# Routed experts in tiles of 256 rows, with the up weights as the standing operand, and a reordered start of the second attention

## The chip, the cores and the metric

The kernel runs on one core of one Trainium2 chip. The metric is the device time of one execution in microseconds; lower is better. The engines of the core are TensorE (PE in the profile, its weight loads PEld), VectorE (DVE), ScalarE (ACT), GpSimd (POOL) and SyncE (SP), which here only issues DMAs.

## What is computed

Two layers of a gated transformer over x of shape (16, 256, 256) in float32. Layer 0 is cross attention and then a mixture of experts; layer 1 is cross attention with a feed-forward part, and then a ternary feed-forward network. The change touches the mixture, and the start of the cross attention behind it. Cut to what matters, the mixture is:

```
scores = softmax(xt @ gate_w.T)            # xt: 4096 tokens x 256, 8 experts
top_vals, top_idx = top_k(scores, 2)
combine = sum(one_hot(top_idx) * top_vals)
for each expert (W1, B1, W2, B2, W3, B3, c):
    h = silu(xt @ W1 + B1) * (xt @ W3 + B3)
    y += c[:, None] * (h @ W2 + B2)
z = (silu(xt @ sw1 + sb1) * (xt @ sw3 + sb3)) @ sw2 + sb2     # shared expert
x = x + tanh(g_ffn[0]) * (y + z)
```

The next line of the reference is the second cross attention on layer-normed x.

## The kernel before

The kernel runs its stages one after another: attention 0, the mixture (`mixture_on_*`), attention 1, its feed-forward part, the ternary network. Each engine has its own hand-written order of steps; engines meet only through semaphores (`wait_ge`, `then_inc`). There is no planner. `paired_blocks` writes a loop: the first block, a hardware loop whose body has two blocks (so that buffers alternate), and the last ones written out.

Products are made exact enough by splitting: each operand is kept as a rounded part `hi` (fp32r) and a residue `lo`, and `product` (its three matmuls per pair are L674, L675 and L676 of the profile) adds hi*hi, lo*hi and hi*lo.

The mixture has two parts. In the shared part all 16 blocks of 256 tokens go through the shared expert, whose weights stand in TensorE while 256 tokens stream. Beside it the routing is worked out: two experts for each token, a place for each of the 8192 pairs in a list sorted by expert, the tokens of each tile (`tokens`, by 64 steps of `place` with tables of zeros and ones, `hot` on VectorE and `tile_values` on ScalarE, L1270), and the expert of each tile.

In the routed part the sorted list is worked off in 72 tiles of 128 rows (`SORTED`), 12 groups of 6 (`GROUP`). Per tile:

- GpSimd gathers 128 rows of normed x with one indirect DMA (L1189), up to 11 tiles ahead, and writes `choice` (L1198), a 128x128 operand that picks the expert's bias rows. It waits for older tiles' output before it overwrites a choice.
- TensorE transposes x (`transpose_x`, L1752), two tiles ahead. `weights` (L1757) loads the expert's column offset into a register. `up` (L1768 is its bias product) has the transposed x as standing operand and streams 512 columns of weights: 1 + 6 products. Then the gated h of the tile before is transposed (`transpose_h`, L1777), and `down` of two tiles before runs: 6 products of 256 columns and a bias product (L1787).
- ScalarE rounds x (L1336), makes silu (L1340), rounds the transposed h (L1344) and writes the output times the row's weight (L1350).
- VectorE makes x's residue (L1620), the gate product (L1631) and h's residue (L1625).
- SyncE stores a group of 6 tiles at once, the last group tile by tile (L1141).

TensorE's order in a group is `up(j)`, `transpose_h(j - 1)`, `transpose_x(j + 2)`, `down(j - 2)`. At the top of each group the loads for two older tiles and for the group's first tile stand in a row.

Attention 1 starts when all rows of `sorted_y` are stored. GpSimd gathers each token's two rows, for the first two blocks the second row into a buffer of its own (L873), which VectorE adds (`add_rows`, L476), and otherwise by adding DMAs into x (L871). A block's second gather waits for its first to land. VectorE takes statistics (L349), GpSimd makes the deviation (L858, L860), VectorE normalises (L366), TensorE transposes (L701). `keys` (L387) and `value_tails` (L397) finish keys and values, and TensorE's transposes of x wait for both the normalised x and the value tails. `late_rows` marks the first block of attention 1, in which the second block's rows are added late.

## Time and profile before

| what | us |
| --- | --- |
| median of 3 runs | 1362.4 (1361.49 to 1372.14) |
| the profiled execution, its own time | 1369.89 |
| its span in the trace | 1368.1 |
| mean granted clock of TensorE | 0.963 of full speed |
| busy: PE, DVE, ACT, POOL | 1221.4, 952.0, 779.3, 641.6 |

All durations in the prediction come from the one profiled execution. Its time is 7.5 us above the median of the three runs. An engine's busy time is the union of its instructions; matmuls overlap each other in the profile, so their pace is read from the distance of their starts.

### The profile page before, as it was taken

How to read it: one execution, taken by the hardware profiler on the slowest of the kernel's cores; microseconds unless marked ns; L12 is line 12 of the kernel's file. 1: busy time of each engine (PE TensorE's matmuls, PEld its weight loads, DVE VectorE, ACT ScalarE, POOL GpSimd, SP SyncE). 2: the span in 40 equal slices, each digit the busy share in tenths (PEclk: the TensorE clock that was granted, in tenths of full speed). 3: DMA queues.
4: the chain of work that ended last, by engine and by line, in shares of the span. 5: the costliest groups of instructions: out<-in, count | busy, mean ns of one | idle time of the engine just before them, and what ended most of it. 6: DMA issues, size and time to landing. Idle time of an engine off the chain costs nothing.

```text
span 1368.1 us, 27370 instructions
## 1 busy us (share of the span) xinstructions
PE 1221.4 (89%) x8822; PEld 1097.0 (80%) x8823; DVE 952.0 (70%) x2124; ACT 779.3 (57%) x1589; POOL 641.6 (47%) x790
## 2 busy tenths in 40 slices
PE   5999999989796899999469999998789999799998
PEld 4888888889795788888458888987678888687877
DVE  5788888766873333333448888887688778888886
ACT  3676777667383344444336777765434445466664
POOL 4333343142104444442377776730335545567776
PEclk9999999989999999999779999999899999899999
DMA  3122112123001332221333334310300000000000
GB/s 94 50 55 63 48 49 51 42 72 117 9 1 47 108 89 88 88 73 54 89 64 64 65 59 72 57 28 5 109 1 0 0 0 1 0 24 24 23 23 31
DMA packets 70041, 66.25 MB, mean 48 GB/s; under 512 B 26080, under 2 KB 62176, under 8 KB 69728
## 3 DMA queue, kind: packets, MB, share of 16 engines
q1 hardware_dynamic: 55264, 44.29, 11.2%
q0 software_dynamic: 12288, 17.83, 6.7%
q10 hardware_dynamic: 2432, 3.41, 0.8%
q8 instruction: 31, 0.51, 0.2%
q14 instruction: 26, 0.21, 0.1%
HBM read 42.43 MB, written 17.83 MB: 44 GB/s over the span
## 4 chain that ended last, share of the span: by engine, by line
PE 67%; DVE 13%; ACT 8%; issue 7%; POOL 3%; DMA 2%; another core or an unknown queue 0%; ACTq 0%; DVEq 0%; POOLq 0%
PE PSUM L674 11%; PE PSUM L676 10%; PE PSUM L675 10%; PE PSUM L746 6%; PE PSUM L725 6%; PE PSUM L734 4%; PE PSUM L689 2%; ACT s_m_xn L1270 2%; PE PSUM L744 2%; PE PSUM L2478 2%; PE PSUM L2479 2%; PE PSUM L701 1%; PE PSUM L1768 1%; PE PSUM L2470 1%; PE PSUM L2459 1%
## 5 line engine op out<-in xcount | busy, mean ns | idle before, releaser
L1930 POOL TENSOR_TENSOR s_f_h_lo<-s_f_h,s_f_h_hi 128x512 fp32r<-128x512 f32 x64 | 87.1, 1369 | 110.9 <-ACT s_f_h_hi L1897 110.8
L1631 DVE TENSOR_TENSOR s_m_h<-PSUM,s_m_h 128x256 f32<-128x256 f32 x72 | 30.6, 425 | 148.1 <-ACT s_m_h L1340 147.1
L746 PEld LDWEIGHTS PSUM<-s_a_v_diagonal,s_a_prob_t 128*128 128x128 f32 x1024 | 127.5, 194 | 0.0
L746 PE MATMUL PSUM<-s_a_v_diagonal,s_a_prob_t 128*128 128x36 f32 x1024 | 126.6, 270 | 0.0
L871 POOL DMA_INDIRECT s_x<-sorted_y,s_slots x60 | 95.2, 1587 | 51.7 <-DMA s_x<-sorted_y,s_slots 36.1
L409 DVE TENSOR_REDUCE s_a_row_max<-PSUM 128x8 f32<-128x640 f32 x128 | 104.3, 815 | 14.1 <-PE PSUM L725 10.4
L1189 POOL DMA_INDIRECT s_m_xn<-normed_x,s_tokens x72 | 70.1, 973 | 89.5 <-DVE s_tokens L1497 77.0
L623 ACT ACTIVATE s_a_prob_t<-PSUM 128x640 f32<-128x640 f32 x128 | 89.5, 699 | 33.6 <-PE PSUM L734 32.9
L416 DVE TENSOR_TENSOR s_a_less<-PSUM,s_a_row_max 128x640 f32<-128x640 f32 x128 | 105.0, 820 | 3.6 <-issue 0.2
L606 ACT ACTIVATE s_a_prob<-s_a_less 128x512 f32<-128x512 f32 x128 | 80.5, 629 | 44.4 <-DVE s_a_less L416 42.0
L725 PE MATMUL PSUM<-s_a_kd,s_a_q_hi 64*128 64x320 f32 x512 | 91.0, 360 | 13.6 <-DVE s_a_q_lo L379 12.7
L1894 ACT ACTIVATE s_f_h<-PSUM,s_cols 128x512 f32<-128x512 f32 x64 | 44.0, 687 | 96.0 <-PE PSUM L676 93.6
L734 PE MATMUL PSUM<-s_ident,s_a_prob 128*128 128x128 f32 x640 | 94.6, 279 | 2.8 <-ACT s_a_prob L607 2.3
L616 ACT ACTIVATE PSUM<-s_a_mask 128x640 f32<-128x640 f32 (+1 forms) x128 | 89.4, 699 | 0.0
L2307 POOL TENSOR_TENSOR s_t_gh<-s_t_h,s_t_g 128x1024 f32<-128x1024 f32 x32 | 78.1, 2442 | 21.7 <-ACT s_t_h L2268 21.7
L883 POOL TENSOR_TENSOR s_x<-s_x,s_a_bias 128x512 f32 (+1 forms) x16 | 20.3, 1270 | 144.5 <-DVE s_a_xn L366 133.9
L1340 ACT ACTIVATE s_m_h<-PSUM 128x256 f32<-128x256 f32 x72 | 27.6, 383 | 98.4 <-PE PSUM L676 89.5
L1198 POOL TENSOR_TENSOR s_m_x_hi<-s_m_bias,s_ones 128x128 fp32r<-128x128 f32 x72 | 28.6, 399 | 115.4 <-PE PSUM L1787 113.6
L674 PE MATMUL PSUM<-s_ffn_hi,s_f_h_hi 128*128 128x256 f32 x256 | 74.0, 289 | 6.7 <-POOL s_f_h_lo L1930 6.6
L734 PEld LDWEIGHTS PSUM<-s_ident,s_a_prob 128*128 128x128 f32 x640 | 76.8, 151 | 3.6 <-issue 3.6
L674 PE MATMUL PSUM<-s_moe_w,s_m_h_hi 128*128 (+1 forms) x208 | 67.7, 325 | 12.4 <-DVE s_x L1517 5.4
L725 PEld LDWEIGHTS PSUM<-s_a_kd,s_a_q_hi 64*128 64x128 f32 x512 | 48.8, 186 | 30.2 <-issue 15.1
(309 smaller groups left out, 4359.3 us busy)
## 6 DMA issues: line engine op xcount, KB each, us to landing
sorted_y<-s_m_xn SPq DMA_DIRECT2D x11, 768.0 KB
s_a_kd<-s_a_k_parts SPq DMA_DIRECT2D x256, 20.0 KB
s_x<-x SPq DMA_DIRECT2D x16, 256.0 KB, 2.7
s_a_ctx<-ctx SPq DMA_DIRECT2D x32, 128.0 KB
s_moe_raw<-moe_w SPq DMA_DIRECT2D x16, 256.0 KB
normed_x<-s_m_xn SPq DMA_DIRECT2D x16, 256.0 KB, 3.3
y<-s_x SPq DMA_DIRECT2D x16, 256.0 KB, 2.1
s_late_raw<-moe_w SPq DMA_DIRECT2D x11, 256.0 KB, 3.0
```

The lines of the kernel that those rows point to most:

```text
L409: dve.tensor_reduce(mx, s, AX.X, ALU.max).then_inc(a.max_done, 1)
L416: dve.tensor_tensor(a.prob[j % 2][:].rearrange("p (c h) n -> p c h n", c=2), s, mx.unsqueeze(3).broadcast_to([P, 2, HPC // 2, CTXP]), ALU. ...
L616: act.activation(a.scores[:, j % 2, :, 0:HPC // 2 * CTXP].rearrange("p c (h n) -> p c h n", n=CTXP), mask.unsqueeze(1).broadcast_to([P, 2, ...
L623: act.activation(a.prob_t[j % 2][:], a.prob_t_ps, ACT.Copy).then_inc(a.pt_done, 1)
L674: pe.matmul(ps, lh, rh, start=start and i == 0, stop=False, skip_group_check=not start)
L675: pe.matmul(ps, ll, rh, start=False, stop=False, skip_group_check=not start)
L676: last = pe.matmul(ps, lh, rl, start=False, stop=stop and i == n - 1, skip_group_check=not start)
L725: last = pe.matmul(ps, queries[i][rows, m, qt * P:(qt + 1) * P], keys[i][rows, m], start=False, stop=i == 2, skip_group_check=True)
L734: last = pe.transpose(a.prob_t_ps[:, c, :], a.pairs[j % 2][:, c, :], ident[:])
L746: last = pe.matmul(a.o_ps[:, 2 * c:2 * c + 2, :], a.prob_t[j % 2][:, c, :], v[:, j // BT, 0, 2 * c:2 * c + 2], start=False, stop=c == PC - ...
L871: last = pool.indirect_dma_start(x[:, tile, :], None, d["sorted_y"], row, compute_op=ALU.add)
L1930: pool.tensor_tensor(f.h_lo[m % 4][:], f.h[m % 4][:], f.h_hi[m % 4][:].bitcast(F32), ALU.subtract).then_inc(f.h_split, 1)
```

## The change

- A routed tile has 256 rows (`BT` = 2 gathers and halves per tile). There are `ROUTED` = 32 + 8 - 1 = 39 tiles, 13 groups of 3 (`GROUP`); tables of half tiles have 78 columns, not 72.
- `copy_up` on VectorE: a register load of the tile's expert, then a copy of its up weights (128 x 2048, hi and lo) into one of two buffers `up_w`. It waits until the product that used the buffer is done.
- `up` now has these weights as standing operand and streams x: 24 products of 256 columns into one of two pairs of PSUM banks. h comes out transposed; `transpose_h` and its steps are gone.
- The bias of up is no longer a product: `up_biases` makes a table for all tiles by four products once, and ScalarE and VectorE add it per partition.
- `down` makes two halves of 6 + 1 products; x, h, and output are rounded and split 256 rows at a time, by the forms that the shared part uses. `choice` serves `down` alone.
- TensorE's order is `transpose_x(j + 1)`, `up(j)`, `down(j - 1)`. Its loop has 6 tiles per turn. ScalarE, VectorE and SyncE have their 39 tiles written out; each tile is stored by itself. Gathers run two tiles ahead; the choice of tile n and the gathers of tile n + 2 alternate.
- The loads of attention 1's weights go out after the fourth tile's store.
- In attention 1 GpSimd splits the second context before the first deviation and issues both gathers of the third block ahead of the first turn. On VectorE `keys` and `value_tails` come ahead of the late rows in the first turn, and the third block's statistics at its end.

TensorE in the hardware loop, around `down`. Before (L674 to L676 with `s_m_x_hi` are up products of 512 columns, with `s_m_h_hi` down products; L1777 transposes h, L1752 x; `s_m_expert` holds the offsets):

```order
L676 MATMUL PSUM<-s_moe_w,s_m_x_hi 128x512
L1774 REGISTER_ALU
L1777 MATMUL PSUM<-s_ident,s_m_h 128x128 x2
L83 REGISTER_ALU
L1752 MATMUL PSUM<-s_ident,s_m_xn 128x128 x2
L674 ISA
L674 MATMUL PSUM<-s_moe_w,s_m_h_hi 128x256
L675 MATMUL PSUM<-s_moe_w,s_m_h_lo 128x256
```

Now (the same products are L677 to L679, `s_m_up_w` is the copied weight):

```order
L677 MATMUL PSUM<-s_m_x_hi,s_m_up_w 128x256
L678 MATMUL PSUM<-s_m_x_hi,s_m_up_w 128x256
L679 MATMUL PSUM<-s_m_x_lo,s_m_up_w 128x256
L1757 ISA
L1757 TENSOR_LOAD s_m_expert
L1757 ISA x2
L1783 REGISTER_ALU
L677 ISA
L677 MATMUL PSUM<-s_moe_w,s_m_h_hi 128x256
L678 MATMUL PSUM<-s_moe_w,s_m_h_lo 128x256
```

Between the last up product and the first down product stood four transposes; now a register load stands there, and the transposes of x follow `down`.

VectorE in a routed tile, before (gate, h's residue, x's residue of one half each):

```order
L1631 TENSOR_TENSOR s_m_h<-PSUM,s_m_h 128x256
L1625 TENSOR_TENSOR s_m_h_lo<-PSUM,s_m_h_hi 128x2x128
L1620 TENSOR_TENSOR s_m_x_lo<-PSUM,s_m_x_hi 128x2x128
L1631 TENSOR_TENSOR s_m_h<-PSUM,s_m_h 128x256
L1625 TENSOR_TENSOR s_m_h_lo<-PSUM,s_m_h_hi 128x2x128
```

Now:

```order
L1611 TENSOR_LOAD s_m_expert
L1611 ISA x2
L1612 ISA
L1612 COPY s_m_up_w<-s_moe_w 128x2048
L1606 TENSOR_TENSOR s_m_x_lo<-PSUM,s_m_x_hi 128x512
L1617 SCALAR_TENSOR_TENSOR s_m_h<-PSUM,s_m_bias,s_m_h 128x256 x2
L1623 TENSOR_TENSOR s_m_h_lo<-s_m_h,s_m_h_hi 128x512
```

A register load and a copy of 2048 elements head each tile's row, ahead of x's residue and the gate; h's residue now reads SBUF, not PSUM.

VectorE in the first turn of attention 1, before (L476 adds the second block's rows, L349 with the following L357 are statistics, L387 and L397 keys and value tails):

```order
L416 TENSOR_TENSOR s_a_less<-PSUM,s_a_row_max 128x640
L476 TENSOR_TENSOR s_x<-s_x,s_z_sum 128x512
L349 BN_STATS s_a_stats<-s_x 128x6 x2
L357 BN_AGGR s_a_mv<-s_a_stats 128x2 x2
L366 TENSOR_SCALAR s_a_xn<-s_x,s_a_mv,s_a_rstd 128x256 x2
L349 BN_STATS s_a_stats<-s_x 128x6 x2
L387 SCALAR_TENSOR_TENSOR s_a_k_parts<-PSUM,s_cols,s_a_k_parts 128x80 x2
L397 TENSOR_TENSOR s_a_v_diagonal<-PSUM,s_headmask 64x2x4x16 x2
```

Now:

```order
L416 TENSOR_TENSOR s_a_less<-PSUM,s_a_row_max 128x640
L387 SCALAR_TENSOR_TENSOR s_a_k_parts<-PSUM,s_cols,s_a_k_parts 128x80 x2
L397 TENSOR_TENSOR s_a_v_diagonal<-PSUM,s_headmask 64x2x4x16 x2
L476 TENSOR_TENSOR s_x<-s_x,s_z_sum 128x512
L349 BN_STATS s_a_stats<-s_x 128x6 x2
L357 BN_AGGR s_a_mv<-s_a_stats 128x2 x2
L366 TENSOR_SCALAR s_a_xn<-s_x,s_a_mv,s_a_rstd 128x256 x2
L409 TENSOR_REDUCE s_a_row_max<-PSUM 128x8
```

Keys and tails moved up before the added rows, and the third block's statistics left this place; they stand at the end of the turn.

The diff, cut to its core:

```diff
-CHOICES = 4
-SORTED = 2 * TILES + EXPERTS
-GROUP = 6
-GROUPS = SORTED // GROUP
+CHOICES = 2
+ROUTED = TILES + EXPERTS - 1
+SORTED = BT * ROUTED
+COLUMNS = ROUTED + ROUTED % 2
+GROUP = 3
+GROUPS = ROUTED // GROUP
...
+                if ahead > 1 and not late_rows:
+                    ln_stats(b.next().next())
+                if ahead:
+                    keys(b.next())
+                if ahead:
+                    value_tails(b.next())
                 if late_rows:
                     add_rows(second)
                     ln_stats(second)
                     ln_aggregate(second)
                     ln_apply(second)
-                if ahead > 1:
-                    ln_stats(b.next().next())
-                if ahead:
-                    keys(b.next())
-                if ahead:
-                    value_tails(b.next())
                 if behind:
...
+                if late_rows:
+                    ln_stats(second.next())
+                    ln_aggregate(second.next())
...
                 gather(first, 1, a.second_rows[0])
+                split_context(second)
                 inverse_std(first)
                 gather(second, 0)
                 gather(second, 1, a.second_rows[1])
-                split_context(second)
                 gather(third, 0)
+                gather(third, 1)
...
-                    gather(third, 1)
...
+            for n in range(ROUTED):
+                sp.wait_ge(m.y_done, SHARED + n + 1)
+                sp.dma_start(sorted_y[:, BT * n:BT * (n + 1), :], m.tile_y[n % 2][:]).then_inc(m.tile_out[n % 2], 16)
+                if n == GROUP:
+                    for i in WA_ORDER:
+                        sp.dma_start(a1.w_raw[:, i], d["wa1"][:, i]).then_inc(a1.w_in[i], 16)
...
+                after(pool, m.t_ps, SHARED + n - 1 if n > 1 else 0)
+                for t in range(BT):
+                    pool.indirect_dma_start(m.tile_x[n % 2][:, t, :], None, d["normed_x"],
+                                            bass.IndirectOffsetOnAxis(ap=tokens[:, BT * n + t:BT * n + t + 1], axis=0)
+                                            ).then_inc(m.tile_in[n % 2], 16)
...
+            gather(0)
+            gather(1)
+            for n in range(ROUTED):
                 choose(n)
+                if n + 2 < ROUTED:
+                    gather(n + 2)
...
+            def output(n):
+                act.wait_ge(m.y_ps, SHARED + n + 1)
+                after(act, m.tile_out[n % 2], 16 * (n // 2))
+                for t in range(BT):
+                    last = act.activation(m.tile_y[n % 2][:, t, :], m.routed_y_bank[n % 2][:, t], ACT.Copy,
+                                          scale=m.tile_weight[:, BT * n + t:BT * n + t + 1])
+                last.then_inc(m.y_done, 1)
+
+            x_rounded(0)
+            for n in range(ROUTED):
+                if n + 1 < ROUTED:
+                    x_rounded(n + 1)
+                activate(n)
+                if n:
+                    output(n - 1)
+                h_rounded(n)
+            output(ROUTED - 1)
...
+            def up_biases():
+                dve.wait_ge(m.logits_ps, BATCH + 2)
+                dve.tensor_copy(m.up_bias, m.up_bias_ps)
...
+            def copy_up(n):
+                after(dve, m.up_done, SHARED + n - 1 if n > 1 else 0)
+                at_expert = dve.value_load(m.expert[0:1, n:n + 1], min_val=EXPERT_COLS, max_val=EXPERTS * EXPERT_COLS)
+                dve.tensor_copy(m.up_w[n % 2][:], m.w[:, bass.ds(at_expert, 4 * MOE_CHUNK)]).then_inc(m.up_copied, 1)
+
+            def gate(n):
+                dve.wait_ge(m.silu_done, SHARED + n + 1)
+                for o in range(KC):
+                    last = dve.scalar_tensor_tensor(m.h[n % 2][:, o], m.routed_up_ps[n % 2][:, 1, o], m.up_bias[:, KC + o, n:n + 1],
+                                                    m.h[n % 2][:, o], ALU.add, ALU.mult)
+                last.then_inc(m.gated, 1)
+
+            def h_residue(n):
+                dve.wait_ge(m.h_round, SHARED + n + 1)
+                dve.tensor_tensor(m.h_lo[n % 2][:], m.h[n % 2][:], m.h_hi[n % 2][:].bitcast(F32),
                                   ALU.subtract).then_inc(m.h_split, 1)
 
+            up_biases()
+            dve.wait_ge(m.late_split, LATE_CHUNKS)
+            copy_up(0)
+            copy_up(1)
+            x_residue(0)
+            for n in range(ROUTED):
+                if n and n + 1 < ROUTED:
+                    copy_up(n + 1)
+                if n + 1 < ROUTED:
+                    x_residue(n + 1)
+                gate(n)
+                h_residue(n)
...
+            def up_biases():
+                pe.wait_ge(m.slots_done, 3)
+                for o in range(4):
+                    last = pe.matmul(m.up_bias_ps[:, o, :], m.bias_parts[:, o * P:(o + 1) * P], m.chosen_r[:], start=True, stop=True)
+                last.then_inc(m.logits_ps, 1)
...
+            def up(g, j):
+                z = (g.z + j) % 2
                 n = GROUP * g.n + j
+                pe.wait_ge(m.up_copied, n + 1)
+                pe.wait_ge(m.t_split, n + 1)
+                after(pe, m.gated, SHARED + n - 1)
+                hi, lo = ([m.up_w[z][:, (2 * k + lower) * MOE_CHUNK:(2 * k + lower + 1) * MOE_CHUNK] for k in range(KC)] for lower in range(2))
+                for gate in range(2):
+                    for o in range(KC):
+                        cut = slice(gate * DIM + o * P, gate * DIM + (o + 1) * P)
+                        last = product(pe, m.routed_up_ps[z][:, gate, o], [(hi[k][:, cut], lo[k][:, cut], m.x_hi[z][:, k], m.x_lo[z][:, k])
+                                                                          for k in range(KC)])
+                last.then_inc(m.up_done, 1)
+
+            def down(g, j):
+                z = (g.z + j) % 2
+                n = GROUP * g.n + j
+                w = weights(g, j)
+                hi, lo = (part(w, 2 * KC + lower).rearrange("p (k c) -> p k c", k=KC) for lower in range(2))
                 pe.wait_ge(m.chosen_done, n + 1)
                 pe.wait_ge(m.h_split, SHARED + n + 1)
+                pe.wait_ge(m.y_done, SHARED + n - 1)
+                for t in range(BT):
+                    tile = slice(t * P, (t + 1) * P)
+                    product(pe, m.routed_y_bank[z][:, t], [(m.h_hi[z][:, k, tile], m.h_lo[z][:, k, tile], hi[:, k], lo[:, k])
+                                                           for k in range(KC)], stop=False)
+                    last = pe.matmul(m.routed_y_bank[z][:, t], m.choice[z][:], m.bias_parts[:, 2 * DIM:], start=False, stop=True)
+                last.then_inc(m.y_ps, 1)
 
             pe.wait_ge(m.x_split, BATCH)
             pe.wait_ge(m.late_split, LATE_CHUNKS)
+            up_biases()
+            transpose_x(Block(0, 0, 0), 0)
 
             def tiles_of(g, behind, ahead):
                 for j in range(GROUP):
+                    at(g, j + 1, behind, ahead, transpose_x)
+                    up(g, j)
+                    at(g, j - 1, behind, ahead, down)
+
+            paired_blocks(pe, GROUPS, tiles_of, 0, 2)
+            down(final_group, GROUP - 1)
```

## Rows read from the trace of the kernel before

**Rows 1.** The page, busy time of each engine over the whole span.

```profile
PE 1221.4 (89%) x8822; PEld 1097.0 (80%) x8823; DVE 952.0 (70%) x2124; ACT 779.3 (57%) x1589; POOL 641.6 (47%) x790
```

**Rows 2.** Timeline of the routed stage's start and end (start us, us, engine, line, operation).

```profile
428.34 0.95 POOL L1189 DMA_INDIRECT s_m_xn<-normed_x,s_tokens  x1 [0.30 <-issue]
...
429.26 0.75 DVE L1517 SCALAR_TENSOR_TENSOR s_x<-PSUM,s_gates,s_x 128x512 f32<-128x512 f32 x1 [2.08 <-PE PSUM L1697]
...
434.92 0.79 PE L1768 MATMUL PSUM<-s_m_bias_parts,s_m_x_hi 128*128 128x512 f32 x1 [3.06 <-POOL s_m_x_hi L1198]
...
664.81 0.47 ACT L1350 ACTIVATE s_m_xn<-PSUM,s_m_bias 128x256 f32<-128x256 f32 x1 [1.38 <-PE PSUM L1787]
```

**Rows 3.** Windows, 540 to 560 us (window: length, busy per engine, clock, DMA share, GB/s).

```profile
540.00:560.00 20.00, 19.57 (x122) 16.97 (x121) 6.69 (x20) 9.29 (x27) 9.67 (x15) 1.00 0.28 90
```

**Rows 4.** Timeline of TensorE, one routed tile at 540 us.

```profile
540.32 0.40 PE L676 MATMUL PSUM<-s_moe_w,s_m_x_hi 128*128 x1
...
541.25 0.38 PE L1777 MATMUL PSUM<-s_ident,s_m_h 128*128 128x128 f32 x2
...
541.47 0.38 PE L1752 MATMUL PSUM<-s_ident,s_m_xn 128*128 128x128 f32 x2
...
541.92 0.28 PE L676 MATMUL PSUM<-s_moe_w,s_m_h_hi 128*128 x1
...
542.40 0.28 PE L1787 MATMUL PSUM<-s_m_bias_parts,s_m_x_hi 128*128 128x256 f32 x1
...
543.21 0.39 PE L676 MATMUL PSUM<-s_moe_w,s_m_x_hi 128*128 x1
```

**Rows 5.** Timeline, idle time before an instruction in the routed stage, in brackets.

```profile
448.87 0.47 ACT L1350 ACTIVATE s_m_xn<-PSUM,s_m_bias 128x256 f32<-128x256 f32 x1 [3.22 <-remote]
...
478.13 0.47 PE L1768 MATMUL PSUM<-s_m_bias_parts,s_m_x_hi 128*128 128x512 f32 x1 [0.43 <-DVE s_m_x_lo L1620]
...
496.96 0.47 PE L1768 MATMUL PSUM<-s_m_bias_parts,s_m_x_hi 128*128 128x512 f32 x1 [1.26 <-POOL s_m_x_hi L1198]
```

**Rows 6.** Timeline of the shared experts' stage: silu, gate, h rounded, h's residue, 256 rows each.

```profile
423.13 0.81 ACT L1253 ACTIVATE s_m_h<-PSUM,s_cols 128x256 f32<-128x256 f32 x2
...
423.98 0.88 DVE L1522 SCALAR_TENSOR_TENSOR s_m_h<-PSUM,s_cols,s_m_h 128x256 f32<-128x256 f32 x2 [3.19 <-ACT s_m_h L1253]
...
424.89 0.63 ACT L1259 ACTIVATE s_m_h_hi<-s_m_h 128x512 fp32r<-128x512 f32 x1 [0.95 <-DVE s_m_h L1522]
...
425.55 0.69 DVE L1528 TENSOR_TENSOR s_m_h_lo<-s_m_h,s_m_h_hi 128x512 fp32r<-128x512 f32 x1 [0.70 <-ACT s_m_h_hi L1259]
```

**Rows 7.** Timeline around 990 us: VectorE's 128x2048 operation, with GpSimd busy and idle.

```profile
988.27 2.20 DVE L2223 TENSOR_SCALAR s_t_code<-s_t_raw 128x2048 fp32r<-128x2048 f32 x1
...
994.15 1.23 DVE L2223 TENSOR_SCALAR s_t_code<-s_t_raw 128x2048 fp32r<-128x2048 f32 x1
...
987.65 1.73 POOL L1930 TENSOR_TENSOR s_f_h_lo<-s_f_h,s_f_h_hi 128x512 fp32r<-128x512 f32 x1 [1.76 <-ACT s_f_h_hi L1897]
```

**Rows 8.** GpSimd's gather and choice: the gather's own answer, the page's group.

```profile
L1189 POOL DMA_INDIRECT s_m_xn<-normed_x,s_tokens x72: 942/969/1200, 426.8 to 622.6; - x72
...
DMA to landing us min/median/max: 3.0/3.0/3.0
...
L1198 POOL TENSOR_TENSOR s_m_x_hi<-s_m_bias,s_ones 128x128 fp32r<-128x128 f32 x72 | 28.6, 399 | 115.4 <-PE PSUM L1787 113.6
```

**Rows 9.** The register load of an expert's offset on TensorE's queue.

```profile
L1757 PEldq TENSOR_LOAD <-s_m_expert x96: 296/301/1240, 431.5 to 662.2; - x96
```

**Rows 10.** Windows with the granted clock (the number before the DMA share).

```profile
448.00:452.00 4.00, 2.41 (x9) 2.32 (x10) 1.09 (x3) 1.77 (x5) 1.77 (x3) 0.50 0.16 52
...
708.00:712.00 4.00, 4.00 (x20) 3.34 (x19) 1.92 (x4) 0.70 (x1) 3.69 (x4) 0.50 0.49 85
```

**Rows 11.** Timeline of the second attention's first turn, TensorE and VectorE.

```profile
704.90 1.09 PE L701 MATMUL PSUM<-s_ident,s_a_xn 128*128 128x128 f32 x4 [11.07 <-DVE s_a_v_diagonal L397]
...
702.96 0.75 DVE L349 BATCH_NORM_STATS2 s_a_stats<-s_x 128x6 f32<-128x256 f32 x2 [5.02 <-DMA s_x<-sorted_y,s_slots]
```

More of the change, by code:

```diff
@@ L984, in __init__ @@
                 self.h_lo = [sb(scope, f"m_h_lo{z}", [P, KC, SEQ], F32R) for z in two]
-                self.tile_x = [self.xn[:, z * GROUP:(z + 1) * GROUP, :] for z in two]
-                self.tile_y = [self.xn[:, (2 + z) * GROUP:(3 + z) * GROUP, :] for z in two]
-                self.choice = [self.x_hi[z // KC][:, z % KC, P:] for z in range(CHOICES)]
                 def by_token(buffer):
@@ L1121, in mixture_on_sync @@
                     load_late(n + 2)
-            def store(g):
-                sp.wait_ge(m.y_done, SHARED + GROUP * (g.n + 1))
-                sp.dma_start(sorted_y[:, bass.ds(GROUP * g.n, GROUP), :], m.tile_y[g.z]).then_inc(m.tile_out[g.z], 16)
-            sp.wait_ge(m.y_ps, SHARED + GROUP)
-            for i in WA_ORDER:
-                sp.dma_start(a1.w_raw[:, i], d["wa1"][:, i]).then_inc(a1.w_in[i], 16)
-            def body(g, behind, ahead):
-                if behind:
-                    store(g.last())
             sp.wait_ge(m.late_split, LATE_CHUNKS)
@@ L1346, in output @@
-            def output(g, j):
-                act.wait_ge(m.y_ps, SHARED + GROUP * g.n + j + 1)
-                if j == 0:
-                    after(act, m.tile_out[g.z], 16 * g.half)
-                act.activation(m.tile_y[g.z][:, j, :], m.y_ps_bank[:, 0], ACT.Copy,
-                               scale=m.group_weight[g.z][:, j:j + 1]).then_inc(m.y_done, 1)
-            act.wait_ge(m.up_done, SHARED)
-            for j in range(AHEAD):
-                x_rounded(Block(0, 0, 0), j)
-            def tiles_of(g, behind, ahead):
-                for j in range(GROUP):
-                    activate(g, j)
-                    at(g, j - 1, behind, ahead, h_rounded)
-                    at(g, j + AHEAD, behind, ahead, x_rounded)
-                    at(g, j - 2, behind, ahead, output)
@@ L1628, in gate @@
-            def gate(g, j):
-                dve.wait_ge(m.silu_done, SHARED + GROUP * g.n + j + 1)
-                h = m.h[j % 2][:, 0]
-                dve.tensor_tensor(h, m.tile_up_ps[:, j % 2, DIM:], h, ALU.mult).then_inc(m.gated, 1)
-            for j in range(AHEAD):
-                x_residue(first, j)
-            def tiles_of(g, behind, ahead):
-                for j in range(GROUP):
-                    gate(g, j)
-                    at(g, j - 1, behind, ahead, h_residue)
-                    at(g, j + AHEAD, behind, ahead, x_residue)
@@ L1761, in part @@
                 return m.w[:, bass.ds(at + n * MOE_CHUNK, MOE_CHUNK)]
-            def up(g, j, w):
+            def up(g, j):
+                z = (g.z + j) % 2
                 n = GROUP * g.n + j
-                pe.wait_ge(m.chosen_done, n + 1)
-                pe.wait_ge(m.t_split, n + 1)
-                ps = m.tile_up_ps[:, j % 2, :]
-                pe.matmul(ps, m.choice_of(g, j), m.bias_parts[:, 0:2 * DIM], start=True, stop=False, skip_group_check=True)
-                product(pe, ps, [(m.x_hi[j % 2][:, k, 0:P], m.x_lo[j % 2][:, k, 0:P], part(w, 2 * k), part(w, 2 * k + 1))
-                                 for k in range(KC)], start=False).then_inc(m.up_done, 1)
@@ L1772, in transpose_h @@
-            def transpose_h(g, j):
-                n = GROUP * g.n + j
-                pe.wait_ge(m.gated, SHARED + n + 1)
-                pe.wait_ge(m.h_split, SHARED + n)
-                for k in range(KC):
-                    last = pe.transpose(m.ht_bank[:, k], m.h[j % 2][:, 0, k * P:(k + 1) * P], ident[:])
-                last.then_inc(m.ht_ps, 1)
-            def down(g, j, w):
-                n = GROUP * g.n + j
-                hi, lo = (part(w, 2 * KC + n).rearrange("p (k c) -> p k c", k=KC) for n in range(2))
-                pe.wait_ge(m.h_split, SHARED + n + 1)
-                pe.wait_ge(m.y_done, SHARED + n)
-                product(pe, m.y_ps_bank[:, 0], [(m.h_hi[j % 2][:, k, 0:P], m.h_lo[j % 2][:, k, 0:P], hi[:, k], lo[:, k])
-                                                for k in range(KC)], stop=False)
-                pe.matmul(m.y_ps_bank[:, 0], m.choice_of(g, j), m.bias_parts[:, 2 * DIM:], start=False, stop=True).then_inc(m.y_ps, 1)
+                pe.wait_ge(m.up_copied, n + 1)
@@ L1789, in mixture_on_tensor @@
             pe.wait_ge(m.x_split, BATCH)
-            pe.wait_ge(m.slots_done, 3)
             pe.wait_ge(m.late_split, LATE_CHUNKS)
-            for j in range(AHEAD):
-                transpose_x(Block(0, 0, 0), j)
+            up_biases()
+            transpose_x(Block(0, 0, 0), 0)
             def tiles_of(g, behind, ahead):
-                offset = {j: weights(g.last(), j + GROUP) for j in (-2, -1) if behind}
                 for j in range(GROUP):
-                    offset[j] = weights(g, j)
-                    up(g, j, offset[j])
-                    at(g, j - 1, behind, ahead, transpose_h)
-                    at(g, j + AHEAD, behind, ahead, transpose_x)
-                    at(g, j - 2, behind, ahead, lambda group, tile: down(group, tile, offset[j - 2]))
```

140 lines of the change are left out of this document (56 added, 84 removed).

## Prediction

> **What bounds the kernel now.** I read the page first, then the stretch of routed tiles by windows, one tile of it in the timeline, the idle gaps of TensorE there, and last the first microseconds of the second attention.
>
> The page says that TensorE is busy 89% of the span [rows 1]. That is a mean over stages with different limits. The change touches the routed stage, from the first up product at 434.92 us to the last row of experts' output at 664.81 + 0.47 = 665.28 us [rows 2], and the start of the second attention. From 540 to 560 us TensorE is busy 19.57 of 20 us, VectorE 6.69, ScalarE 9.29 and GpSimd 9.67 [rows 3]: the stage is bound by TensorE's stream, and the other three have more than half their time free.
>
> One routed tile of 128 rows, in the timeline: the same product of two tiles starts at 540.32 and 543.21, so a tile takes 2.89 us [rows 4]. The busy times of single matmuls overlap, so I count distances of starts. From 540.32 to 541.25 TensorE starts four products of 512 columns, 0.232 us each; from 541.92 to 542.40 four of 256, 0.12 each (0.1175 over longer runs); from 541.25 to 541.47 is 0.22 us for a pair of transposes. Seven wide products (1.62), seven narrow ones (0.82) and two pairs of transposes (0.44) make 2.88 us, which agrees. 72 such tiles are 207.7 us. The stage lasts 230.4. The other 22.7 us are gaps and low clock: some 3 us in which TensorE waits for an output of ScalarE that starts at 448.87 after 3.22 us of waiting, 1.26 and 0.43 us at the starts of groups, where three register loads stand in a row (496.96 and 478.13 stand for twelve such places, some 9 us in all) [rows 5], a stretch at half clock before and after, and the drain.
>
> **The change, part by part.**
>
> *TensorE's work per tile.* A tile now has 256 rows and there are 39 instead of 72. Up: 4 output parts x 6 products of 256 columns = 24; down: 2 x 7 = 14; x transposed: 4 transposes; no h transposes and no bias product with the up part. 38 x 0.1175 + 0.44 = 4.91 us per tile, x 39 = 191.4 us (less 0.9 for two sets of transposes ahead of the first product: 190.6). Against 207.7 this is -17.1 us. Most of it is transposes (4 per 128 rows before, 2 now) and the bias products; the column count hardly moves, since 78 half tiles stand where 72 stood.
>
> *Does another engine become the bound?* With T the tile time, E the end of up(n) on TensorE, and durations from [rows 6]: silu of two halves 0.81 us ends at E+0.9; gate 0.88 ends at 1.8; ScalarE must first put out tile n-1, which waits for down(n-1) (E+1.65) and takes 0.9, so h is rounded from 2.7 to 3.3; h's residue 0.69 ends at 4.1. down(n) starts on TensorE at E+4.91, so 0.8 us are spare. Then VectorE goes on: weight copy, x residue 0.69, next gate. VectorE's own ring is copy + 0.69 (x) + 0.88 (gate) + 0.10 + 0.63 + 0.10 (wait for the rounding on ScalarE) + 0.69 (h) = copy + 3.1 us.
>
> *The copy.* 2048 elements per partition, SBUF to SBUF, and the trace of before has no such copy. Nearest rows: a TENSOR_SCALAR of 128x2048 with fp32r output takes 1.23 us at 994.15, when GpSimd is idle, and took 2.20 at 988.27, when it started while GpSimd's TENSOR_TENSOR ran until 989.38 [rows 7]. I take 1.23, the row without company. [...] With 1.23 the ring is 4.33 us, below 4.91. [...]
>
> GpSimd's share: one choice 0.40 and two gathers of 0.97 with 0.3 between, 2.9 us per tile, and it starts a gather for tile n+2 as soon as tile n is transposed. Landing takes 3.0 us [rows 8], so both are there 0.5 + 1.27 + 3.0 = 4.8 us later, and are used about 9.4 us later. This cover of 4.6 us also holds if each is pushed by a whole copy. In the steady state the second gather of a pair ends at about E+4.4 and the copy is due at E+4.1: it may lose 0.3 us. Ring: 4.6.
>
> *Register loads on VectorE.* A load of the expert's offset costs TensorE's sequencer 0.30 us and some register steps after it [rows 9]; TensorE hides one per tile behind queued matmuls. On VectorE it comes while the h residue (0.69) still runs. I take 0 exposed, bound 0.5. With that bound the ring is 5.1 us. TensorE's own load now stands before down, one per tile and not three in a row, so the gaps of [rows 5] shrink to that of the loop branch. I take 0.4 x 5 turns of the loop = 2 us instead of the 9.
>
> *Start.* Tile 0 needs two gathers instead of one. The second starts at 428.34 and lands at about 431.4; transposes, 0.63, 0.69 give 433.5. VectorE is busy with add(15) until 430.0 [rows 2], then the biases (0.2), two loads and two copies (2 x 1.23 + 0.5), so x's residue ends near 434.1 and up(0) starts at about 434.4: 0.5 earlier than now, where it waits for the choice on GpSimd. After this pause the clock is at its half level (the product at 434.92 takes 0.79 us [rows 2], and one later in the stage 0.40 [rows 4]); that costs 1.5 us as now.
>
> *The stall before 449.6.* ScalarE waits 3.22 us for something the profile calls remote [rows 5], then the granted clock is 0.50 for a while [rows 10]; together 3.0 + 2.6 = 5.6 us. Nothing in the code asks for it. ScalarE's code is now straight instead of a loop, so it may go or come again elsewhere. In the sum against the profiled run I let 2 us return.
>
> *End.* After the last up product: h chain 4.1, less down(37) 1.65, is 2.4 us exposed, then down(38) 1.65 and the output 0.94 + 0.2.
>
> Sum: 434.4 + 190.6 + 1.5 (clock) + 0.5 (first turns) + 2 (loop) + 2.4 + 1.1 (last output) + 2 = 634.5 us, against 665.28: -30.8 us. The last store is twice as large (256 KB): +0.4. In the shared stage, the one-hot tables grow from 72 to 78 columns, on VectorE, ScalarE and in 64 products: +0.7.
>
> *Second attention.* Now TensorE stands idle 11.07 us until 704.90 [rows 11]. It waits for the value tails; these stand on VectorE behind statistics of the third block, which wait 5.02 us for a gather, and this gather stands on GpSimd behind the second block's normalisation. In the new order keys and tails come right after the scores (about 694.6) and the statistics at the end of the turn. What is late next: x of the second block. GpSimd now issues the third block's second gather before the second's deviation, and must wait for the landing of the first: 693.7, two times 1.86 gives 697.1; deviation 1.0; bias 1.25 until 699.3; then VectorE normalises 0.73, and transposes start at 700.2. That gives -4.7. Later the third block's statistics come at about 714.3, deviation until 715.3, where now the normalisation is at 717.9: there only 2.6 are left. I take -3.5 (bounds -2 and -7, the latter if the shorter pause also shortens the half clock around 708 us [rows 10]).
>
> Total: -30.8 + 0.4 + 0.7 - 3.5 = -33.2 us. The profiled run took 1369.9 us (span 1368.1), the median of three is 1362.4, with two runs at 1361.5 and 1362.4. The 5.6 us stall is the most irregular thing in the profile and about as large as this difference; if the faster runs lack it, the change cannot take it from them. I count half: 1362.4 - 33.2 + 3.8 = 1333.
>
> **Rivals.**
>
> A. VectorE's ring is a little too long (register load and waits for gathers exposed): T = 5.1 to 5.3, so + 0.2 to 0.4 x 39 = 8 to 15 us: about 1345. For: the ring is only 0.3 to 0.6 below T. Against: each exposed part must occur on every tile.
>
> [...]
>
> [...]
>
> D. The loop does what it says, but the half clock appears inside it, since stalls come back as at 449: two such stalls more cost 11 us: 1344.
>
> **How the numbers follow.** Forecast 0.62, A 0.18, B 0.08, C 0.04, D 0.08. Differences above 1% (13.6 us) can be told from none. Faster by over 1% (below 1348.8): the forecast, A, D and a part of B, 0.88. Within 1%: the rest of B and a very late A, 0.08. Slower: 0.04. Range: low end, the stall gone in full, the clock better in the attention, 1333 - 10 = 1323; high end between A and B, 1350.
>
> **What would show it.** Right: tiles 4.9 us apart on TensorE, VectorE's copy 1.2 us, VectorE about 3.6 us busy per tile; no wait of TensorE for x_lo or h_lo; TensorE's pause before the second block's transposes 6 us instead of 11. [...] Were tiles 4.9 us apart and the total still above 1350, the loss would be after 665 us.

## The result and the profile after

The changed kernel takes 1356.9 us in the median of 20 runs (1354.6 to 1361.7), the kernel before 1362.1 beside it (20 runs). The ratio is 0.9957, 95% interval 0.9941 to 0.9972: 5.2 us faster by the medians, where 29 were forecast, and 7 us above the top of the range. The profiled run has its own time 1357.3 us and a span of 1355.5.

The page's busy row, to compare with [rows 1], and its group of the gathers, to compare with [rows 8]:

```profile
PE 1213.1 (89%) x9168; PEld 1112.4 (82%) x9169; DVE 1005.4 (74%) x2105; ACT 783.4 (58%) x1535; POOL 654.6 (48%) x751
...
L1182 POOL DMA_INDIRECT s_m_tile_x<-normed_x,s_tokens x78 | 98.7, 1265 | 93.4 <-DVE s_tokens L1477 75.8
```

TensorE has 8 us less to do and the share is the same 89%, so something now leaves it idle. A gather takes 1265 ns on GpSimd instead of 973. The window of [rows 3] now reads:

```profile
540.00:560.00 20.00, 18.38 (x153) 17.77 (x152) 13.12 (x20) 9.40 (x22) 10.87 (x11) 1.00 0.37 103
```

TensorE is idle 1.6 of 20 us in a stretch in which it was idle 0.4; no other engine is busy more than 13.1. So it is a wait, not a new bound. The list of waits from 430 to 655 us names it (who waited for whom; us in total, times, longest; only waits over 0.15 us are listed):

```profile
POOL s_m_choice L1188 <- PE PSUM L1789: 86.9, 37, 6.5
...
PE PSUM L1752 <- DMA s_m_tile_x<-normed_x,s_tokens: 17.7, 23, 2.6
```

TensorE's transposes of x (L1752) wait 23 times for gathered rows. One of these waits, 1.9 us, comes before the first product; 22 waits, 15.8 us, are inside the loop. The timeline of one tile, all engines, shows where they begin:

```profile
542.78 0.28 PE L1789 MATMUL PSUM<-s_m_bias_parts,s_m_choice 128*128 128x256 f32 x1
...
543.15 0.40 POOL L1188 TENSOR_TENSOR s_m_choice<-s_m_bias,s_ones 128x128 fp32r<-128x128 f32 x1 [1.54 <-PE PSUM L1789]
543.54 0.65 PE L1752 MATMUL PSUM<-s_ident,s_m_tile_x 128*128 128x128 f32 x4 [0.47 <-DMA s_m_tile_x<-normed_x,s_tokens]
543.69 0.98 POOL L1182 DMA_INDIRECT s_m_tile_x<-normed_x,s_tokens  x1
...
544.98 1.59 POOL L1182 DMA_INDIRECT s_m_tile_x<-normed_x,s_tokens  x1 [0.30 <-issue]
545.22 1.23 DVE L1612 CAST s_m_up_w<-s_moe_w 128x2048 fp32r x1
...
549.39 0.65 PE L1752 MATMUL PSUM<-s_ident,s_m_tile_x 128*128 128x128 f32 x4 [0.68 <-DMA s_m_tile_x<-normed_x,s_tokens]
```

Read it from top to bottom. Down of tile n-2 ends (542.78 + 0.28). Only then does GpSimd make the choice of tile n (543.15), and behind it, in its order, the two gathers of tile n+2 (543.69, 544.98). The second runs beside VectorE's copy and takes 1.59 us instead of 0.98. The transposes at 543.54 are those of tile n+1. Those of tile n+2 (549.39) need the rows just gathered and wait 0.68 us. The gathers were free to start when the transposes of tile n had ended, near 538.6; they started 5 us later, because an instruction with another reason to wait stood ahead of them.

The stage now goes from its first up product to its last output at 653.89 + 0.84 = 654.73 us:

```profile
433.72 0.55 PE L677 MATMUL PSUM<-s_m_x_hi,s_m_up_w 128*128 128x256 f32 x1 [0.43 <-issue]
...
653.89 0.84 ACT L1335 ACTIVATE s_m_tile_y<-PSUM,s_m_bias 128x256 f32<-128x256 f32 x2 [4.20 <-PE PSUM L1789]
```

That is 221.0 us, where before had 230.4 [rows 2] and the prediction 200.1 (634.5 less 434.4). The second attention's pause, which was 11.07 us [rows 11]:

```profile
690.03 1.11 PE L704 MATMUL PSUM<-s_ident,s_a_xn 128*128 128x128 f32 x4 [6.09 <-DVE s_a_xn L366]
```

### The profile page after: what moved, and what is told of

It is laid out like the page before. It is cut to its first block, busy times and chain, and to the rows that moved or that the text cites. A ratio compares the mean times of both kernels' runs of the same rounds, so it can differ in the third digit from the quotient of the medians.

```text
span 1355.5 us, 27131 instructions
## 1 busy us (share of the span) xinstructions
PE 1213.1 (89%) x9168; PEld 1112.4 (82%) x9169; DVE 1005.4 (74%) x2105; ACT 783.4 (58%) x1535; POOL 654.6 (48%) x751
## 4 chain that ended last, share of the span: by engine, by line
PE 60%; DVE 12%; ACT 7%; issue 7%; DMA 7%; POOL 5%; ACTq 0%; SPq 0%; DVEq 0%; POOLq 0%
PE PSUM L677 10%; PE PSUM L679 9%; PE PSUM L678 9%; PE PSUM L749 6%; PE PSUM L728 6%; DMA s_m_tile_x<-normed_x,s_tokens 5%; PE PSUM L737 4%; PE PSUM L692 2%; ACT s_m_xn L1252 2%; PE PSUM L747 2%; PE PSUM L2474 2%; PE PSUM L2475 1%; PE PSUM L704 1%; PE PSUM L758 1%; POOL s_m_tile_x L1182 1%
## 5 line engine op out<-in xcount | busy, mean ns | idle before, releaser
L1182 POOL DMA_INDIRECT s_m_tile_x<-normed_x,s_tokens x78 | 98.7, 1265 | 93.4 <-DVE s_tokens L1477 75.8
L677 PE MATMUL PSUM<-s_m_x_hi,s_m_up_w 128*128 128x256 f32 x312 | 92.2, 296 | 0.4 <-issue 0.4
L679 PE MATMUL PSUM<-s_m_x_lo,s_m_up_w 128*128 128x256 f32 x312 | 88.9, 285 | 0.0
L678 PE MATMUL PSUM<-s_m_x_hi,s_m_up_w 128*128 128x256 f32 x312 | 88.9, 285 | 0.0
L677 PE MATMUL PSUM<-s_ffn_hi,s_f_h_hi 128*128 128x256 f32 x256 | 73.9, 289 | 6.6 <-POOL s_f_h_lo L1926 6.6
L1323 ACT ACTIVATE s_m_h<-PSUM,s_m_bias 128x256 f32<-128x256 f32 x78 | 32.7, 471 | 75.3 <-PE PSUM L679 75.3
L677 PE MATMUL PSUM<-s_moe_w,s_m_h_hi 128*128 (+1 forms) x220 | 64.9, 295 | 10.1 <-DVE s_x L1503 5.3
```

What stands on the lines that cost most here:

```text
L677: pe.matmul(ps, lh, rh, start=start and i == 0, stop=False, skip_group_check=not start)
L678: pe.matmul(ps, ll, rh, start=False, stop=False, skip_group_check=not start)
L679: last = pe.matmul(ps, lh, rl, start=False, stop=stop and i == n - 1, skip_group_check=not start)
L1182: pool.indirect_dma_start(m.tile_x[n % 2][:, t, :], None, d["normed_x"], bass.IndirectOffsetOnAxis(ap=tokens[:, BT * n + t:BT * n + t + 1] ...
```

## The experiments

Three theories. W: the choice's wait holds back the gathers behind it. L: beside VectorE's copy the second gather takes 1.59 us instead of 0.98 (called the lock here), and this makes it late. D: the landings themselves are late (up to 6.3 us, 3.4 in the median), because stores and loads stand in the DMA engines.

The kernel before, run beside each kernel, was not always equally fast: 1368.4 us beside e1 to e4, 1362.8 beside r_after, r_gather_first, e5 and e6, 1366.6 beside r2 and e7 to e9. Only times within one of these three groups are compared to a microsecond.

**Gathers ahead of the choice (e1).**

```diff
             for n in range(ROUTED):
-                choose(n)
                 if n + 2 < ROUTED:
                     gather(n + 2)
+                choose(n)
```

> The changed kernel with the gathers of tile n+2 ahead of the choice of tile n on GpSimd; nothing else. Theory W (waiting in line: the choice waits for the end of down(n-2), and the gathers behind it in GpSimd's order begin only there, 5.4 us before they are needed, in a tile time of 5.03): gathers start at the end of the transposes of tile n, some 4.5 us earlier; TensorE's waits for the gathered rows, 15.8 us in 22 places after the first tile, go to under 2 us, all tiles stand 5.03 us apart, the whole is 14 to 16 us faster than the changed kernel, about 1342 us. Theory D (the landings themselves are late, up to 6.3 us, since stores and loads of weights stand in the DMA engines): only the short waits go, the long ones (2.6, 1.5, 1.8 us) stay, 8 us faster, 1349. Theory L (the second gather is 0.6 us longer beside VectorE's copy, and this makes the waits): its length of 1.6 us stays, and the gain is also there, since the cover is longer; e2 tells L from W.

Measured: 1335.8 us, ratio to before 0.9768 (0.9738 to 0.9797). Waits of TensorE for gathered rows inside the loop: none. The gathers now follow the transposes, and from the fourth tile on all tiles stand 4.96 us apart (timeline, first GpSimd, then TensorE):

```profile
542.23 0.40 POOL L1188 TENSOR_TENSOR s_m_choice<-s_m_bias,s_ones 128x128 fp32r<-128x128 f32 x1 [1.55 <-PE PSUM L1789]
542.85 0.98 POOL L1182 DMA_INDIRECT s_m_tile_x<-normed_x,s_tokens  x1 [0.22 <-PE PSUM L1752]
544.13 1.50 POOL L1182 DMA_INDIRECT s_m_tile_x<-normed_x,s_tokens  x1 [0.30 <-issue]
...
541.98 0.60 PE L1752 MATMUL PSUM<-s_ident,s_m_tile_x 128*128 128x128 f32 x4
...
546.94 0.60 PE L1752 MATMUL PSUM<-s_ident,s_m_tile_x 128*128 128x128 f32 x4
```

The second gather is still 1.50 us long and nobody waits for it. It went further than W's 14 to 16 us; a direct comparison follows below.

**No copies (e2).** From the third tile on only 4 of the 2048 columns are copied, so the output is wrong in part.

```diff
-                dve.tensor_copy(m.up_w[n % 2][:], m.w[:, bass.ds(at_expert, 4 * MOE_CHUNK)]).then_inc(m.up_copied, 1)
+                width = 4 * MOE_CHUNK if n < 2 else 4
+                dve.tensor_copy(m.up_w[n % 2][:, 0:width], m.w[:, bass.ds(at_expert, width)]).then_inc(m.up_copied, 1)
```

> The changed kernel with its order on GpSimd, but from the third tile on the copy of the up weights is 4 columns wide instead of 2048 (the weights of the first two tiles are used for all, so the output of the experts is left wrong in part). Theory L: the second gather of each tile falls from 1.59 to 0.98 us and lands 0.6 us sooner; the short waits of TensorE (0.3 to 0.7 us, 19 of them) vanish, of the long ones 4 to 5 us stay: about 11 us faster than the changed kernel, 1346 us. Theory W alone (the lock has no part): the second gather stays at 1.59 or, where it shortens, waits shrink by no more than 3 us. If VectorE's ring were the bound (rival A of the prediction) the tile time of tiles that do not wait would fall below 5.03 us; I expect it to stay at 5.03.

Measured: 1350.3 us, ratio 0.9873 (0.9843 to 0.9902). The changed kernel did not run beside it (elsewhere 1356.9 and 1358.1), so the gain is read from the profiled runs: from the first up product to the end of the last output 213.9 us instead of 221.0, so 7 us. Gathers from 540 to 640 us take 1009 ns, and of the waits from 440 to 640 us these are left:

```profile
L1182 POOL DMA_INDIRECT s_m_tile_x<-normed_x,s_tokens x34 | 34.3, 1009 | 7.6 <-issue 5.2
...
PE PSUM L1753 <- DMA s_m_tile_x<-normed_x,s_tokens: 10.5, 11, 2.8
```

Half the waits went, those left are longer, and the tiles without a listed wait still take 5.0 to 5.1 us, nearly all. So L is a part: it took the last 0.5 us of a cover that was nearly nothing. By itself it does not make the waits, since 10.5 us of them are left without it. The 11 us expected were too many, since the chain down, choice, gathers, landing still closes with hardly a margin.

**The changed kernel and the gathers-first kernel side by side.**

> The changed kernel again, beside the others on one chip. The first four runs had a chip on which the kernel before took 1368 us instead of 1362; the changed kernel's ratio to before was 0.9957 elsewhere. I expect 0.994 to 0.997 of before; the old attention order (0.9938 in its run) would otherwise look faster than the new.

> The gathers ahead of the choice, again, now beside the changed kernel on the same chip: 20 to 25 us faster than it (waits 15.8, tile time 4.96 instead of 5.03 for 38 tiles 2.7, half clock after the long wait 1.3, and what the earlier start gives). If the 32 us against before were a matter of the chip, the ratio to before would come back to about 0.985.

Measured: 1358.1 us (ratio 0.9971, 0.9953 to 0.9989) and 1333.6 us (0.9795, 0.9761 to 0.9828) beside 1362.8 for before. The order of two lines is worth 24.5 us. In these profiled runs the stage's last output starts 23.8 us earlier:

```profile
630.72 0.84 ACT L1335 ACTIVATE s_m_tile_y<-PSUM,s_m_bias 128x256 f32<-128x256 f32 x2 [2.88 <-PE PSUM L1789]
```

**The copy made twice (e5).** With the gathers first:

```diff
+                dve.tensor_copy(m.up_w[n % 2][:], m.w[:, bass.ds(at_expert, 4 * MOE_CHUNK)]).then_inc(m.up_first, 1)
+                dve.wait_ge(m.up_first, n + 1)
                 dve.tensor_copy(m.up_w[n % 2][:], m.w[:, bass.ds(at_expert, 4 * MOE_CHUNK)]).then_inc(m.up_copied, 1)
```

> The gathers ahead of the choice, and each tile's copy of the up weights made twice (the second waits for the first, then both are the same): what VectorE's ring has to spare. By the prediction's ring (4.33 us without waits, 4.6 with the wait for a gather) the tile time becomes 5.6 to 5.9 us instead of 4.96, 25 to 37 us slower than with one copy. If the ring has more to spare than the prediction says (VectorE's waits of 0.5 and 1.06 us per tile are slack in full), it stays under 5.3 us, under 13 us slower. [...]

Measured: 1359.7 us, 26 more than with one copy. From 440 to 640 us TensorE waits for x's residue, which stands behind the copies on VectorE, and VectorE itself is idle 0.3 us before each first copy, where the register load stands:

```profile
DVE s_m_up_w L1613 <- issue: 8.8, 32, 0.5
PE PSUM L677 <- DVE s_m_x_lo L1607: 7.2, 20, 0.5
```

VectorE's ring is then the bound. The transposes of one tile and the next stand 5.2 to 5.8 us apart, 5.53 in the mean of 32 tiles (456.39 to 633.31), and the second copy adds 1.26 us to the ring (542.47 to 543.73), so the ring with one copy is about 4.3 us: the 4.33 without waits, below the 4.6 with them. The timeline also shows the lock from both sides, GpSimd's gathers first, then VectorE's copies:

```profile
541.55 2.27 POOL L1183 DMA_INDIRECT s_m_tile_x<-normed_x,s_tokens  x1 [0.30 <-issue]
...
547.00 0.95 POOL L1183 DMA_INDIRECT s_m_tile_x<-normed_x,s_tokens  x1 [0.30 <-issue]
...
542.47 1.23 DVE L1613 CAST s_m_up_w<-s_moe_w 128x2048 fp32r x1 [0.33 <-issue]
...
548.03 1.23 DVE L1613 CAST s_m_up_w<-s_moe_w 128x2048 fp32r x1 [0.30 <-issue]
```

The first gather meets a copy before it is done and ends at 543.82, 0.12 us behind the copy's end (543.70). The second is done at 547.95, before its copy starts, and takes 0.95. The copy is 1.23 in both cases.

**The weight loads of attention 1 later (e6).** In the changed kernel:

```diff
-                if n == GROUP:
+                if n == 15:
```

> The changed kernel with the four loads of attention 1's weights after the 16th tile's store instead of the 4th's. Theory D for the longest wait: the gather issued at 460.62 us landed after 6.3 us because the four loads of 256 KB were issued at 460.01. Then the wait of 2.6 us at 466.96 goes to a short one (0.4 us) and a wait of about 2.6 us appears 12 tiles later, near 525 us; the whole stays the same within 2 us. If the long wait has another cause it stays at 466.96.

Measured: 1359.3 us, as the changed kernel (1358.1 beside it). The long wait left 466.96 us (the wait nearest to it, at 468.94, is 0.82) and came back behind the loads, which now go out at 524.53 (SyncE's queue, then TensorE):

```profile
524.53 1.91 SPq L1136 DMA_DIRECT2D s_a_w_raw<-wa  x4
...
531.91 0.48 PE L1752 MATMUL PSUM<-s_ident,s_m_tile_x 128*128 128x128 f32 x1 [3.66 <-DMA s_m_tile_x<-normed_x,s_tokens]
```

So D is shown for the single longest wait. Three waits of 0.9, 1.5 and 1.8 us at 495.5, 593.0 and 638.6, whose gathers landed late too (after 4.4, 4.5 and 5.6 us), were not tried by themselves. And a late landing needs a short cover to do harm: in r_gather_first the gather that starts at 460.17 lands after 6.3 us, and nobody waits for it. In the changed kernel the gather that started 0.6 us behind the four loads of 256 KB landed after 6.3 us, the median one after 3.4. How loads and gathers share the DMA engines was not shown.

**The order of attention 1.** Undone in the changed kernel (e3), alone in the kernel before (e4), and undone with the gathers first (e7, beside r2, the kernel that it starts from). The edit is the part of the diff on attention 1, backward or alone.

> The changed kernel with the order of before in attention 1 (both engines: rows, statistics, keys and tails on VectorE; context split, gathers of the third block on GpSimd). My theory: 3 to 4.5 us slower than the changed kernel, since TensorE's pause before the second block's transposes is 11 us again instead of 6.0: about 1360.5 us. Rival: the time comes back later in the attention, and the order is worth under 1 us.

> The kernel before with the new order of attention 1 alone. My theory: 3 to 4.5 us faster than before (1358.5 us), which leaves only about 2 us of the measured 5 to the whole change of the routed tiles in the median, although the routed stage is 10.5 us shorter in the profiled runs: the profiled run of before was 8 us above its median. Rival: the order is worth under 1 us, and the routed tiles gave all 5.

> The gathers ahead of the choice, once more, only as the kernel that the other three of this call start from: 0.976 to 0.981 of before.

> The gathers ahead of the choice, with the order of before in attention 1. The two runs on this order disagree (undoing it in the changed kernel 0 to 3 us by the medians, 1 us behind the last output in the profiled runs; alone in the kernel before 4.9 us, 3.6 us in the profiled runs). My prediction's term was 3.5 (2 to 7). If it holds, this kernel is 3 to 4.5 us slower than the one it starts from; if most of it is given back in later blocks, 0.5 to 1.5 us slower.

Measured: e3 1359.8 (ratio 0.9938, 0.9917 to 0.9960), e4 1364.4 (0.9964, 0.9949 to 0.9979), r2 1335.9 (0.9772, 0.9747 to 0.9797), e7 1336.9 (0.9783, 0.9764 to 0.9801). The changed kernel did not run beside e3, which looks better than it by the ratio and 1.7 to 2.9 us worse by the time: this pair says nothing to 0.3%. Two pairs ran side by side: e4 is 3.9 us faster than before (1368.4), r2 is 1.0 us faster than e7. The traces of e7 and r2 show where the gain goes:

```profile
672.17 1.09 PE L701 MATMUL PSUM<-s_ident,s_a_xn 128*128 128x128 f32 x4 [11.01 <-DVE s_a_v_diagonal L397]
...
690.03 0.66 PE L701 MATMUL PSUM<-s_ident,s_a_xn 128*128 128x128 f32 x4
...
705.67 0.66 PE L701 MATMUL PSUM<-s_ident,s_a_xn 128*128 128x128 f32 x4
```

```profile
668.75 1.12 PE L704 MATMUL PSUM<-s_ident,s_a_xn 128*128 128x128 f32 x4 [6.09 <-DVE s_a_xn L366]
...
688.56 0.63 PE L704 MATMUL PSUM<-s_ident,s_a_xn 128*128 128x128 f32 x4 [0.78 <-DVE s_a_v_diagonal L397]
...
704.78 0.66 PE L704 MATMUL PSUM<-s_ident,s_a_xn 128*128 128x128 f32 x4
```

These are the transposes of the second, third and fourth block, old order (e7), then new (r2). From the end of the last output (632.61 and 633.50) they start after 39.6, 57.4 and 73.1 us in the old order and 35.3, 55.1 and 71.3 in the new: a gain of 4.3, then 2.4, then 1.8 us, and at the end of the span 0.3. Before and e4 give 4.3 us at the second block and 3.6 at the end. Over all profiled runs, the time from the end of the last output to the end of the span is 699.0 to 700.8 us in the ten with the new order (mean 700.0; e9 left out) and 700.9, 701.7 and 702.9 in the three with the old one (mean 701.8). So the order is worth something, about 1.8 us by the means; single pairs scatter from 0.3 to 3.6.

**No copies, with the gathers first (e8).** The edits of e1 and e2 together.

> The gathers ahead of the choice, and from the third tile on copies of 4 columns (weights of the first two tiles used for all, so part of the experts' output is wrong). What copy and lock cost once the gathers have their cover: nothing. The second gather falls from 1.50 to 0.98 us, the tile time stays 4.96 us, the whole the same within 2 us. If the copies still cost (a VectorE ring that is nearly the bound), tiles come to 4.9 us or less and the whole is 3 us or more faster.

Measured: 1334.1 us, 0.9766 (0.9745 to 0.9787), beside 1335.9 for r2. Tiles stand 4.96 us apart, as with copies; the gathers fell to one length:

```profile
L1182 POOL DMA_INDIRECT s_m_tile_x<-normed_x,s_tokens x70 | 67.9, 970 | 19.8 <-issue 10.7 <-PE PSUM L1753 9.1
```

Once the gathers have their cover, copy and lock cost nothing that can be measured (1.8 us between the medians, while the five runs of each kernel spread over 5 to 8 us).

**A bias added between two gathers (e9).** In attention 1, with the gathers first:

```diff
                 gather(third, 0)
+                add_bias(first)
                 gather(third, 1)
...
-                if a.stage == 1 and not behind:
-                    add_bias(first)
```

> The gathers ahead of the choice, and in attention 1 GpSimd adds the first block's bias between the two gathers of the third block, while it waits 2.6 us for the first of them, instead of behind the second block's deviation, where VectorE's normalisation waits for it. The second block's transposes start 1.2 to 1.7 us earlier, the pause before them falls from 6.1 to about 4.5 us; 1 to 2 us faster at most, which the times alone can hardly show.

Measured: 1334.3 us, 0.9761 (0.9736 to 0.9785), beside 1335.9. The pause before the second block's transposes is 4.79 us instead of 6.09, near the 4.5 expected; the times alone can't tell it from nothing. No kernel of these runs beats the gathers ahead of the choice by more than that.

## Why the prediction was wrong

| | forecast | changed kernel | gathers first (e1) |
|---|---|---|---|
| first up product | 434.4 | 433.72 | 432.22 |
| tile time without a wait | 4.91 | 5.02 | 4.96 |
| listed waits for gathers in the loop | 0 | 15.8 | 0 |
| first up product to end of last output | 200.1 | 221.0 | 200.3 |
| pause before second block's transposes | 6 | 6.09 | 6.13 |
| median of all runs | 1333 | 1356.9 | 1335.8 |

*The step that failed* is GpSimd's share: "it starts a gather for tile n+2 as soon as tile n is transposed", with landing 4.8 us later, use 9.4 us later and "this cover of 4.6 us". I read the gather's own condition and not what stands ahead of it on its engine. The choice of tile n waits for down(n-2), one up and one down behind the transposes of tile n. From there to the landing are 0.1 + 0.4 + 0.14 (543.06 to 543.69), 1.29 to the second gather, 3.4 to its landing (median): 5.3 us, and the rows are due after 5.0. The cover of 4.6 us was -0.3. A tile that waits 0.4 us gives the next one as much more time, so waits of 0.3 to 0.7 come on about every second tile (intervals 5.0 and 5.5 to 5.6); with four longer ones that is the 15.8 us. [Rows 8] had shown the choice of before idle 113.6 us behind TensorE's product L1787, so the wait was in sight. In the kernel before it held nothing back, since gathers ran many tiles ahead.

That one step carries the miss: with it undone, 1333.6 and 1335.8 us against a forecast of 1333. The traces also say where the time lies. From the transposes of the third tile to those of the last are 201.0 us in the changed kernel and 178.9 in e1, 22.1 less. The listed waits are 15.8 of them. Each of the 22 costs some 0.2 more than its entry (a tile with an entry of 0.47 takes 5.59, not 4.96 + 0.47), 4.1 in all; after a wait the four transposes take 0.41 instead of 0.35 us, which is the whole difference between tiles of 5.02 and 4.96, 0.7 in all for the tiles that don't wait; the half clock behind the longest wait (granted 0.52 from 467 to 470 us) costs 1.4.

That e1 met the forecast so closely is in part luck. In its stage of 200.3 us for 200.1 the 2 us for the loop and the 2 us for the stall did not come, and 38 x 0.05 us of tile time, some 0.7 more than forecast at the start (granted clock 0.50 from 432 to 436 us) and 1.3 of half clock at the end (0.57 from 628 to 632) made up for them. Another run of the same kernel (r_gather_first), without that half clock (1.00 from 628 to 632) and with less of it at the start (0.51 from 434 to 436, then 1.00), has a stage of 197.5 us.

The other steps:
- TensorE's work, 4.91 us a tile: 4.96. The transposes with the first product behind them take 0.56 us, as forecast (0.44 + 0.12). The rest lies in the up products: from the second to the last of a tile 22 steps take 2.62 us, 0.119 each where the sum has 0.1175.
- The copy, 1.23 us: 1.23 in nearly all of 39, the longest 1.46. Right. B in the chances, and in the upper end of the range (1350), stands for a copy of 2.3 us; no run shows one. The copy's register load was taken at 0 and costs next to nothing here (VectorE is idle ahead of 3 of the 39 copies, 1.2 us in all); the 0.3 us of e5 show only where VectorE is the bound.
- VectorE's ring, 4.33 to 4.6: about 4.3, by the doubled copy. Right, and rival A is out: no tile waits for a copy (0.8 us once).
- The lock. I put its price on the copy, as 0.3 us of VectorE's ring. It fell on the other side: the second gather takes 1.58 to 1.60 us instead of 0.98 on nearly every tile, and one of the 39 copies is longer (1.46 us at 524.38, where the gather takes 1.04). "This cover also holds if each is pushed by a whole copy" would have been true of a cover of 4.6.
- The stall, "I let 2 us return", as irregular: wrong twice. The profiled run of e4, with the routed part of before, has it again (3.21 us at 445.98) and the same 230.4 us of stage, so it belongs to that code; none of it is in the changed kernel. So taking half of the profiled run's 7.5 us above the median for it had no ground, though it came out near.
- Register loads at the loop's turns, 2 us: none to be seen; with the gathers first 4.96 holds through all turns.
- The end: 2.4 us of exposed h chain are there (2.32), but after it, in the profiled run of the changed kernel, the last down part runs at half clock (granted clock 0.60 from 650 to 654 us), products 0.21 us apart instead of 0.12, 1.3 us. In its second profiled run (r_after, granted clock 1.00 from 650 to 654 us) and in one of three with the gathers first (r_gather_first, 1.00 from 628 to 632) it did not.
- Second attention: the pause of 6 is 6.09 and the -4.7 at the second block -4.3; -3.5 in the whole is about -1.8 by the means above, and 0.3 to 3.6 by the pairs. A part of the gain is given back in the blocks behind, as the prediction said, but more of it than the 1.2 us it took off.

C in the chances stands for tiles of 6.9 us, with each copy behind a whole gather. No run shows that: tiles without a wait took 5.02 us, and the copy started beside a running gather, which took 0.6 us longer. Rival D's half clock inside the loop came once in the changed kernel, behind the longest wait (transposes at 466.96, next tile 6.33 us; granted clock 0.52 from 467 to 470 us). In e6 it moved with that wait (0.50 from 532 to 535, 1.00 from 467 to 470). Behind the waits of 1.5 and 1.8 us at 593.0 and 638.6 the changed kernel's clock was 1.00.

## What to carry to other kernels

For a DMA that is to be hidden, add up the time from the last instruction *ahead of it on its engine*, whatever that one waits for, and not from its own condition. A small operation that is due late, put in front of a prefetch, takes the prefetch's whole lead (here 4.6 us by the forecast, -0.3 as measured); putting the prefetch first cost nothing here. A wait of a few tenths on every second step is worth looking for: between the two orders TensorE's busy share differs by one point (89 and 90% of the span), the time by 24 us.

## What was not expected of the hardware

A gather on GpSimd beside VectorE's fp32r copy of 2048 columns ended just behind the copy, as three pairs show: started 0.24, 0.16 and 0.92 us before the copy, it ended 0.12, 0.11 and 0.12 us after the copy's end (546.57 and 546.45; 545.63 and 545.52; 543.82 and 543.70), though it needs 0.98 us in all. By this count the first two had 0.74 and 0.82 us of work left when the copy began, and all but 0.12 us of it ran beside the copy. In all three the gather began first, and the copy still took the 1.23 us that it takes without one. One pair of the changed kernel went the other way: the gather that starts at 523.77 took 1.04 us, and the copy that starts 0.61 us behind it 1.46. What decides between the two was not shown. For a 128x2048 operation beside a plain GpSimd TENSOR_TENSOR, [rows 7] had shown the other side, VectorE waiting: 2.20 us instead of 1.23.
